# The routing stage of a graph and expert layer: gate weights held still, logits turned back, sums added from SBUF

## The reference, cut to what matters

```python
x = x + segment_sum(layernorm(x)[src].astype(f16) * w16[:, None], ...)   # "agg", float16
h = layernorm(x)                          # x: 50000 tokens of 256 numbers, float32
logits = h @ gate_w + gate_b              # gate_w: 256 x 8
idx = argmax(softmax(logits)); prb = its probability
pos = (cumsum(one_hot(idx), axis=0) * one_hot(idx)).sum(-1) - 1
kept = pos < C                            # C tokens fit an expert's queue
y = relu(h[idx's queue] @ w1 + b1) @ w2 + b2      # 8 experts, 256 -> 1024 -> 256
x = x + y * prb * kept
```

## Time and profile before

| | us |
|---|---|
| median of the runs shown | 3347.46 |
| the runs | 3349.5, 3329.72, 3347.46 |
| the profiled execution, its own time | 3333.12 |
| its span, first to last instruction | 3331.5 |
| mean granted TensorE clock, share of full | 0.888 |

### The profile page before, as it was taken

How to read it: one execution, slowest core, us unless ns; L and a number is a source line. 1 busy time by engine, 2 the same in 40 slices (tenths; PEclk the granted TensorE clock), 3 DMA queues, 4 the chain that set the end, 5 groups by cost and what they waited for, 6 DMA issues and landing times.

```text
span 3331.5 us, 65456 instructions
## 1 busy us (share of the span) xinstructions
PE 2816.7 (85%) x20366; PEld 2561.6 (77%) x20367; DVE 2358.6 (71%) x6042; ACT 1626.2 (49%) x2915; POOL 1857.5 (56%) x1680
## 2 busy tenths in 40 slices
PE   5743323279989994999999999999999999999998
PEld 4732323268878884899999999899999999999998
DVE  7944334377766754878778777878877787778777
ACT  3422112145655652555655565565555555565554
POOL 7788888757766675536445333635443354336433
PEclk9766666677877876999999999999999999999999
DMA  9644443377666632212112111211211121111111
GB/s 376 201 76 66 76 88 53 44 293 240 240 223 216 241 119 62 79 42 70 51 41 74 45 48 44 69 42 36 77 51 47 43 68 51 45 41 47 46 50 45
DMA packets 182250, 322.10 MB, mean 97 GB/s; under 512 B 97649, under 2 KB 124348, under 8 KB 166256
## 3 DMA queue, kind: packets, MB, share of 16 engines
q0 software_dynamic: 89696, 146.98, 17.1%
q1 hardware_dynamic: 92288, 172.66, 15.2%
q10 hardware_dynamic: 144, 1.05, 0.1%
HBM read 186.52 MB, written 138.79 MB: 98 GB/s over the span
## 4 chain that ended last, share of the span: by engine, by line
PE 55%; DVE 3%; issue 2%; POOL 1%; DMA 1%; ACT 0%; DVEq 0%; SPq 0%; POOLq 0%; ACTq 0%
PE u_Y L1371 27%; PE u_H L1354 26%; PE u_T L1336 2%; DVE hn L1255 0%; DVE yo L1308 0%; POOL wlo L1134 0%; DVE yo L1311 0%; DVE y L1294 0%; DVE low L1299 0%; DVE hlo L1274 0%; DMA u_x<-out_x,u_rec 0%; DMA raw<-in_L_ffn_w 0%; POOL u_x L1149 0%; DVE y L1288 0%; POOL whi L1130 0%
## 5 line engine op out<-in xcount | busy, mean ns | idle before, releaser
L1149 POOL DMA_INDIRECT u_x<-out_x,u_rec x380 | 412.3, 1085 | 770.5 <-DMA u_rec<-slots 647.1
L1371 PE MATMUL u_Y<-whi,hhi 128*128 128x256 f32 x2784 | 783.6, 281 | 6.9 <-DVE hlo L1274 6.4
L1225 ACT ACTIVATE hm<-u_H,b1e 128x512 f32<-128x512 f32 (+1 forms) x736 | 489.3, 665 | 597.6 <-PE u_H L1354 593.8
L1371 PE MATMUL u_Y<-whi,hlo 128*128 128x256 f32 x2784 | 774.9, 278 | 0.0
L1371 PE MATMUL u_Y<-wlo,hhi 128*128 128x256 f32 x2784 | 774.9, 278 | 0.0
L1274 DVE TENSOR_TENSOR hlo<-hm,hhi 128x512 fp32r<-128x512 f32 (+1 forms) x736 | 463.2, 666 | 190.1 <-ACT hhi L1229 185.6
L1354 PE MATMUL u_H<-xhi,whi 128*128 128x512 f32 (+1 forms) x1472 | 564.5, 384 | 8.8 <-issue 8.8
L1175 POOL DMA_INDIRECT out_x<-yo,u_token x348 | 385.9, 1109 | 322.1 <-DVE yo L1313 252.8
L1354 PE MATMUL u_H<-xlo,whi 128*128 128x512 f32 (+1 forms) x1472 | 557.4, 379 | 0.0
L1354 PE MATMUL u_H<-xhi,wlo 128*128 128x512 f32 (+1 forms) x1472 | 556.7, 378 | 0.0
L1371 PEld LDWEIGHTS u_Y<-whi,hhi 128*128 128x128 f32 x2784 | 527.3, 189 | 10.3 <-DVE hlo L1274 10.2
(11 more groups left out here) (154 smaller groups left out, 4906.0 us busy)
## 6 DMA issues: line engine op xcount, KB each, us to landing
x<-in_x SPq DMA_DIRECT2D x49, 1024.0 KB, 9.2
out_x<-x SPq DMA_DIRECT2D x49, 1024.0 KB, 4.9
agg<-zeros SPq DMA_DIRECT2D x25, 1024.0 KB
at<-agg SPq DMA_DIRECT2D x49, 512.0 KB, 5.7
raw<-in_L_ffn_w POOLq DMA_DIRECT2D x14, 1024.0 KB, 6.6
src_row<-in_src SPq DMA_DIRECT2D x25, 512.0 KB, 5.1
slots<-rec,slot_i POOLq DMA_INDIRECT x392
u_x<-out_x,u_rec POOLq DMA_INDIRECT x380
```

The costliest lines, as they stand in the source:

```text
L1149: pool.indirect_dma_start(out=x1[:, s, :], out_offset=None, in_=out[:, :], in_offset=bass.IndirectOffsetOnAxis(ap=rec[:, s, TOKEN:TOKEN + ...
L1225: act.activation(hm[:, f, cols], ps_H[:, f % 2, cols], ACT.Relu, bias=b1e[:, f:f + 1])\
L1371: last = pe.matmul(ps_Y[:, s, 0:D], a[:, f, rows], w2_at(w, buf, f), start=(f == 0 and j == 0), stop=(f == KF - 1 and j == 2))
```

## The change

- `aggregate`, its PSUM tensor `ps_A`, and the float16 identity go. DVE's `add` reads `at` from SBUF, so both of its inputs now lie in SBUF. SP's load of `at` waits for the addition instead of for `aggregate`.
- `gate(k)` holds `gw` (8 columns) in the array and streams 256 columns of `hT` through it, twice (KD = 2), into `ps_G`, 8 partitions by 1024. ACT `add_bias` adds the bias while it copies `ps_G` to SBUF as `across`, in two halves. PE `turn_back` transposes `across`, 8 blocks of 8x128, into `ps_L`, from which `choice` reads as before. `add_bias` and `turn_back` of step s-1 stand in the bodies of step s.
- `ps_T` has four banks instead of two, so each `turn(k)` has one of its own.
- Both `fill`s and the bias matmul go.
- In PE's body all four `turn`s now come ahead of the `gate`s, and `rank` stands ahead of the last `gate`.
- In ACT's body `deviation` of the next step stands ahead of the `normalise`s, and the four copies follow at the end.
- In DVE's body `scales` of the next step stands first instead of last.

```diff
-    gb = sb("gb", [P, E], F32)
-    ident16 = sb("ident16", [P, P], F16)
+    gb = sb("gb", [E, 1], F32)
+    across = sb("across", [E, STEP], F32)
...
-    ps_A = ctx.enter_context(nc.psum_tensor("ps_A", [P, G, D], F32))
-    ps_T = ctx.enter_context(nc.psum_tensor("ps_T", [P, 2, 4, P], F32))
+    ps_T = ctx.enter_context(nc.psum_tensor("ps_T", [P, 4, 4, P], F32))
+    ps_G = ctx.enter_context(nc.psum_tensor("ps_G", [E, STEP], F32))
...
-                    sp.wait_ge(agg_up, s + 1 - AGGS)
+                    sp.wait_ge(x1_ready, s + 1 - AGGS)
...
+            def add_bias(i, r):
+                s = RING * i + r
+                if not (isinstance(i, int) and s < 1):
+                    act.wait_ge(logits_ready, s)
+                for half in range(2):
+                    act.wait_ge(gated, BANKS * s + 2 * half + 2)
+                    part = slice(half * (STEP // 2), (half + 1) * (STEP // 2))
+                    act.activation(across[:, part], ps_G[:, part], ACT.Identity, bias=gb[:, 0:1])\
+                        .then_inc(across_ready, 1)
...
                 number(i, r)
+                if not (isinstance(i, int) and s in (0, LAST)):
+                    deviation(*next_of(i, r))
                 act.wait_ge(norm_ready, s + 1)
...
-                    if k == 0 and not (isinstance(i, int) and s < 1):
-                        act.wait_ge(gated, s)
+                    if not (isinstance(i, int) and s < 1):
+                        act.wait_ge(gated, BANKS * (s - 1) + k + 1)
                     act.wait_ge(turned, BANKS * s + k + 1)
                     part = slice(k * PER_BANK, (k + 1) * PER_BANK)
-                    act.activation(hT[:, part, :], ps_T[:, k % 2], ACT.Copy).then_inc(hT_ready, 1)
+                    act.activation(hT[:, part, :], ps_T[:, k], ACT.Copy).then_inc(hT_ready, 1)
...
                 normalise(0)
                 normalise(1)
-                if not (isinstance(i, int) and s == LAST):
-                    deviation(*next_of(i, r))
-                copy(0)
+                if isinstance(i, int) and s == 0:
+                    deviation(0, 1)
+                if not (isinstance(i, int) and s < 1):
+                    add_bias(*before_of(i, r, 1))
                 normalise(2)
-                copy(1)
                 normalise(3)
-                copy(2)
-                copy(3)
+                for k in range(BANKS):
+                    copy(k)
             deviation(0, 0)
...
-            def aggregate(i, r):
-                s = RING * i + r
-                pe.wait_ge(agg_loaded[r % AGGS], 16 * ((RING // AGGS) * i + r // AGGS + 1))
-                if not (isinstance(i, int) and s == 0):
-                    pe.wait_ge(x1_ready, s)
-                for g in range(G):
-                    last = pe.matmul(ps_A[:, g, :], ident16[:], at[:, r % AGGS, g, :], start=True, stop=True)
-                last.then_inc(agg_up, 1)
...
                 pe.wait_ge(hT_ready, BANKS * s + k + 1)
-                if k == 0:
-                    if not (isinstance(i, int) and s < 1):
-                        pe.wait_ge(hot_ready, s)
-                    pe.matmul(logits, ident[:], gb[:].unsqueeze(1).broadcast_to([P, G, E]),
-                              start=True, stop=False, skip_group_check=True)
-                for g in range(k * G // BANKS, (k + 1) * G // BANKS):
-                    for kd in range(KD):
-                        last = pe.matmul(logits[:, g, :], hT[:, g * KD + kd, :], gw[:, kd, :],
-                                         start=False, stop=(kd == KD - 1), skip_group_check=True)
-                if k == BANKS - 1:
-                    last.then_inc(gated, 1)
-            def fill():
-                for _ in range(FILL):
-                    pe.matmul(unread, ones[:], before[:].unsqueeze(1).broadcast_to([P, 3, P]),
-                              start=False, stop=True, skip_group_check=True)
+                if not (isinstance(i, int) and s < 1) and k % 2 == 0:
+                    pe.wait_ge(across_ready, 2 * (s - 1) + k // 2 + 1)
+                part = hT[:, k * PER_BANK:(k + 1) * PER_BANK, :].rearrange("p (g kd) c -> p kd g c", kd=KD)
+                wide = STEP // BANKS
+                for kd in range(KD):
+                    last = pe.matmul(ps_G[:, k * wide:(k + 1) * wide], gw[:, kd, :], part[:, kd],
+                                     start=(kd == 0), stop=(kd == KD - 1))
+                last.then_inc(gated, 1)
+            def turn_back(i, r):
+                s = RING * i + r
+                pe.wait_ge(across_ready, 2 * (s + 1))
+                if not (isinstance(i, int) and s < 1):
+                    pe.wait_ge(hot_ready, s)
+                pe.nop(nofuse=True)
+                for g in range(G):
+                    last = pe.transpose(logits[:, g, :], across[:, g * P:(g + 1) * P], ident[0:E, 0:E])
+                last.then_inc(logits_ready, 1)
...
             def turn(i, r, k):
                 s = RING * i + r
                 q = r % 2
                 pe.wait_ge(h_ready, BANKS * s + k + 1)
-                if not (isinstance(i, int) and s < 1 and k < 2):
-                    pe.wait_ge(hT_ready, BANKS * s + k - 1)
+                if not (isinstance(i, int) and s < 1):
+                    pe.wait_ge(hT_ready, BANKS * (s - 1) + k + 1)
                 for n in range(PER_BANK):
                     g, kd = divmod(k * PER_BANK + n, KD)
-                    last = pe.transpose(ps_T[:, k % 2, n, :], h[:, q, g, kd * P:(kd + 1) * P], ident[:])
+                    last = pe.transpose(ps_T[:, k, n, :], h[:, q, g, kd * P:(kd + 1) * P], ident[:])
                 last.then_inc(turned, 1)
             def body(i, r):
                 s = RING * i + r
+                first = isinstance(i, int) and s == 0
                 turn(i, r, 0)
                 turn(i, r, 1)
-                if isinstance(i, int) and s == 0:
-                    aggregate(0, 2)
-                else:
+                if not first:
+                    turn_back(*before_of(i, r, 1))
+                turn(i, r, 2)
+                turn(i, r, 3)
+                gate(i, r, 0)
+                gate(i, r, 1)
+                gate(i, r, 2)
+                if not first:
                     rank(*before_of(i, r, 1))
-                    fill()
-                gate(i, r, 0)
-                turn(i, r, 2)
-                gate(i, r, 1)
-                turn(i, r, 3)
-                if not (isinstance(i, int) and s == 0):
-                    fill()
-                gate(i, r, 2)
-                if not (isinstance(i, int) and s > LAST - 3):
-                    aggregate(*((i, r + 3) if r + 3 < RING else (i + 1, r + 3 - RING)))
                 gate(i, r, 3)
...
-                v.wait_ge(agg_up, s + 1)
+                v.wait_ge(agg_loaded[r % AGGS], 16 * ((RING // AGGS) * i + r // AGGS + 1))
                 v.wait_ge(x_loaded[r], 16 * (i + 1))
-                v.tensor_tensor(x1[:, r], ps_A[:], x1[:, r], ALU.add).then_inc(x1_ready, 1)
+                v.tensor_tensor(x1[:, r], at[:, r % AGGS], x1[:, r], ALU.add).then_inc(x1_ready, 1)
...
-                v.wait_ge(gated, s + 1)
+                v.wait_ge(logits_ready, s + 1)
                 v.tensor_reduce(top[:], logits, AX.X, ALU.max).then_inc(chosen, n.inc())
...
                 two_on = (i, r + 2) if r + 2 < RING else (i + 1, r + 2 - RING)
+                if not (isinstance(i, int) and s == LAST):
+                    scales(*next_of(i, r))
                 if not (isinstance(i, int) and s < 1):
                     choice(*before_of(i, r, 1))
...
                     slot(*before_of(i, r, 1))
-                if not (isinstance(i, int) and s == LAST):
-                    scales(*next_of(i, r))
```

15 lines of the change are left out of this document (7 added, 8 removed).

## The result

The changed kernel took 3348.04 us in the median of 20 runs (3344.87 to 3352.94), the kernel before 3334.68 (3308.63 to 3350.66, 20 runs): 1.0041 of the time, 95% interval 1.0026 to 1.0056. Its profiled execution took 3348.11. I had forecast 3384 with a range from 3350 to 3416, so the time lies just under the range: the sign was right, the size more than three times too large.

A forecast was written before the change was run, and what follows sets the result against it. Bound: a ring through one step, 11.6 us at full clock, 12.8 by PE at half. 46 steps of 12.2, 21 and 6.5 made 589 in place of 547.7; with POOL's 3, 3377 to 3391, middle 3384 (range 3350 to 3416).

The forecast's parts named there:

- With half of the time at each, as now, it is 12.2: Routing stage's mean step: 11.6 us at full clock and 12.8 at half, mixed as in the kernel before.
- the ring: Chain through one step: statistics, `deviation`, `normalise`s, bias, `turn_back`, `choice`, addition, next statistics; 11.6 us at full clock, 12.4 at half.
- 3 for POOL: Routing stage: 3 us added for stretches in which POOL is later than the producers of its slot numbers.
- the clock rises or the gates are cheap: Rival: all steps at full clock take 11.6, about 3353 us; or cheap gates, 3375 us; chance 0.17.
- The gates: PE's 16 streamed matmuls a step at half clock: between 3.4 and 10.2 us, middle 6.8 taken.
- The start: Step 0's `slot` waits behind DVE's addition and its later `rank`: 6.5 us, taken once.
- The addition's duration: DVE's addition with both inputs in SBUF stays about 2.28 us, with 0 to 0.5 more a step possible.
- 1.0 to 2.28 us a step, 1.64 in the mean: POOL's slot-number read waits this long for the two-input addition's end, making POOL's step 11.9 us (11.3 to 12.5).
- The last two steps: Routing stage's last two bodies, without an addition: 10.7 us each, 21 together.
- The clock falls for longer: Rival: PE is granted 1.2 GHz nearly always, steps take 12.8 us, about 3410 us in all; chance 0.15.
- The ring does not hold: Rival: statistics come early enough that ACT never waits; about 3290 us, or 3365 with POOL's blocked reads; chance 0.06.
- POOL is the bound: Rival: additions at a fixed phase to POOL's reads make POOL need 12.5 us a step, 3397 us; chance 0.12.

The follow-up runs named there:

- f1: Kernel before without PE's `aggregate` products, a one-SBUF-input reduction replacing DVE's addition (edges' sums left out): 3413 us, 1.0252 of the kernel before, first kind of chip (before 3333).
- f2: Changed kernel with two groups of seven unread products a step put back on PE: 3388 us, 1.0172 of the kernel before (3333 there).
- a3: Changed kernel with `deviation` behind the bias additions and the addition in four instructions: 3544 us, 0.9867 of the kernel before (3597 on that second-kind chip).
- g4: Changed kernel with the addition in four instructions and `deviation` behind the bias additions, on another second-kind chip: 3489 us, 0.9859 of the kernel before (3531 there).
- a2: Changed kernel with the addition split into four instructions: 3543 us, 0.9847 of the kernel before (3597 on that second-kind chip).
- d2: Changed kernel with the addition split into eight instructions: 3534 us, 0.9835 of the kernel before (3595 on that second-kind chip).

## Why the prediction was wrong

**The failed step** is "With half of the time at each, as now, it is 12.2". It took two lengths, 11.6 at full clock and 12.8 at half, the latter because PE's own work would end the step there, and the mixture of the kernel before. Measured were 11.2 to 11.7 in every regular step; PE's work ended none of them. PE's sum at half clock was not the error: by starts at half clock its `turn`s take 4.0 us, `turn_back` 0.9, `rank` 0.8 and the `gate`s 6.9, which is 12.6. What was wrong is to take the clock as one level through a step. In the changed kernel it falls and rises within each (0.71 to 0.85), so PE is busy for 9.0 to 10.4 us of most steps and the ring ends them. With the ring's own 11.6 in all 46 steps the forecast's sum would be 534, 21 and 6.5, or 561.5, against 556.3 measured; of the 33 us that it was too high, 28 are this term. The rest of the 36 us between 3384 and 3348 is 7 from the base (the three runs shown had a median of 3347.46, and I took the middle between it and the profiled execution; the 20 runs have 3334.68) and 3 for POOL, less 6 for POOL's late end and what lies elsewhere.

That 11.6 fits so well in the sum is in part luck. The regular steps are 11.37 in the mean, which in 46 steps is 10.6 us less than 11.6; the three turns of the loop, for which the forecast had no term, give 9.4 of it back.

The rival "the clock rises or the gates are cheap" has this length too, 3353 us, but its condition, full clock in all steps, did not come: 0.79 over the stretch. That the mixture must not be carried over is what f1 shows most plainly: the clock went from 0.77 to 0.54 with less work on PE.

**What held.** The ring: forecast 11.6, by rows 11.24, with the hand-overs as listed; ACT idle ahead of L614 and DVE ahead of L831, once a step. The terms that were off: `turn_back` with its hand-over (0.66, not 1.13), the bias additions with theirs (1.38, not 1.18) and the hand-over from DVE to ACT (0.04, not 0.13). At half clock the ring was forecast 0.8 longer, by `turn_back` alone; it is `turn_back` alone, but 0.36. The gates: at half clock their weight loads start 0.43 us apart, so 16 make 6.9, and the middle value of 6.8 stands. The start: 18.3 us for the first interval, 7.1 above a regular one, for 6.5. The addition's duration: 2.29 for 2.28.

**POOL.** The mechanism of the held read held, but "1.0 to 2.28 us a step, 1.64 in the mean" took the reads to fall anywhere in the addition. They don't: a held DMA ends some 0.85 us behind the addition, and so sets the phase of the next eight. The hold is the ring's step less 10.3 us, 1.17 in the mean. In f2's step of 11.77 the hold was 1.05 (2.03 for 0.98), and POOL waited 0.47 beyond its 0.30 before another DMA: hold and wait together fill what the longer ring leaves. By this it costs nothing as long as the ring is longer than 10.3.

**The last two steps** were forecast at 10.7 each and took 9.33 and 7.58, 4.5 us less; POOL, which can't follow them, gave 5.4 us of it back at the end.

**The rivals.** "The clock falls for longer" did not happen in the changed kernel, but in f1, with less work on PE. "The ring does not hold" is refuted by the waits. "POOL is the bound" is refuted for the first chip by its trace (nobody waits for POOL, its holds follow the ring, and the steps follow `turn_back`'s 0.36), and by f2 only as far as a longer ring made longer steps.

The Trainium skill (SBUF — State Buffer, Who interferes with whom) says that VectorE with two SBUF inputs contends with a GpSimd read and with one input does not. The runs agree with both halves: 437.4 and 448.1 us of POOL's time with two inputs, 383.5 with one and 383.8 from PSUM. By the lock above, POOL without holds would be worth some 5 us in the changed kernel on the first chip, its late end; that is an estimate that no run measured.

**A version that beats both?** On the second kind a3 and g4, which keep the whole computation, are 1.3 and 1.4% faster than the kernel before, a2 and d2 1.5 and 1.6%; none of them was measured on the first kind.

## What to carry to other kernels

Do not average step lengths over the clock's two levels with the shares of the old kernel: work out each engine's sum, ask which length holds if the clock changes within the step, and count in a chain only the TensorE work that stands on it. Work taken off TensorE can come with a lower clock and a longer time, as in f1; look at the granted clock after every such edit. Follow the waits once around a step before adding up engines: a chain that closes through one step sets its length, here 11.2 us, with PE busy for 9.8 of it and the others for less, and a contention beside it may only fill time that was free.
